# A four-block attention and feed-forward kernel on Trainium2: layer 6's context products between layer 5's stages, and layer 5's last two stages among layer 6's first softmax units

## The chip, the cores and the metric

The kernel is one program on one core of a Trainium2 chip. The metric is the device time of one execution in microseconds. Engines are named as in the profile: PE (TensorE, with PEld for its weight loads), DVE (VectorE), ACT (ScalarE), POOL (GpSimd) and SP (SyncE, which here only issues transfers). Each engine runs its own instructions strictly in the order in which the program lists them, and waits at semaphores for the others.

## What is computed

Four blocks act on x (4 x 512 x 128, fp32) and a context (4 x 77 x 128). Each adds a gated attention and then a gated feed-forward part; the kernel numbers these eight parts as layers 0 to 7. The change lies between layer 5 and layer 6:

```
# layer 5: three cycles of a small network on LN(x), all per sequence
gf  = global_net(mean over rows of LN(x))
out = LN(x)
for _ in range(3):
    tf = sigmoid(gelu(gelu(gelu(out@w1+b1)@w2+b2)@w3+b3)@w4+b4)   # stages 0 to 3
    out = out + (0.1 + ar*(0.7*gf + 0.3*tf - 0.5)*2) * twist(out) # stage 4 and couple
x = x + tanh(g) * out
# layer 6: attention with 16 heads of 8 channels on the 77 context rows
Q = LN(x)@wq.T + bq;  K = ctx@wk.T + bk;  V = ctx@wv.T + bv
x = x + tanh(g) * (softmax(mask(Q K.T / sqrt(8))) V @ wo.T + bo)
```

K and V of layer 6 depend on the context alone, not on x.

## The kernel before, in words

The four sequences are worked on in two passes of the whole program ("pairs"), with two sequences s = 0 and 1 in each. Activations are held as four tiles of 128 rows per sequence.

**The list of steps.** schedule() (line 127) writes out one list of steps by hand. Every engine runs through that list in order and issues its own part of each step, so the place of a step in the list is its place on every engine. No cost or due time is computed anywhere.

**PSUM slots.** Products land in six slots: S0 and S1 (two banks each), T0 and T1, G0 and G1 (one bank each); in the code they are 0 to 5. Four rotors (line 116) hand them out in the order of the list: `big` gives S0, S1 in turn, `turn` T0, T1, `gen` G0, G1, and `wide` S0, S1, T0, T1. The rotors do not know of each other. On TensorE `take(i)` (line 734) waits until all earlier contents of slot i have been read out:

```python
            def take(i):

                used[i] += 1
                pe.wait_ge(*free[i].value(used[i]))
```

**Layer 5.** cycle(s, n) (line 351) is stage n % 5 of cycle n // 5 of sequence s, written (s, cycle, stage) below. Stages 0 to 3 are, for each half of 256 columns, one product (two fp32 instructions) and one ScalarE activation. Stage 4 is the product for the twist over all 512 columns, followed by `couple` on VectorE for both halves: three operations of 256 columns each (lines 1816, 1818, 1824), which update `cur` = `kh`, a tile with both sequences' state. The two sequences run interleaved, the second seven stages behind: the loop at line 372 issues stage n of sequence 0 and stage n - 7 of sequence 1 for n = 4 to 21. cycle_out transposes the result back, and VectorE adds it to x. Then norm_stats, norm_apply and norm_turn of layer 6 normalise x and transpose it.

**Layer 6's products.** project_context(6, s) multiplies the context with the keys' weights into a `gen` slot (two instructions of 77 columns) and a repeated context with the values' weights into a `big` slot (five products, ten instructions). VectorE evicts the keys with their bias (line 1777) and the values in two multiplications by a 0/1 block pattern (line 1780), whose second frees the big slot; GpSimd spreads the keys by head (line 1383). project_queries(6, s) is one product of 512 columns and one VectorE eviction (line 1799). Before, the keys of sequence 0 went into `qh` and those of sequence 1 into `kh`, that is into layer 5's state of sequence 0, so that they had to come after its last use.

**The units.** small_attention (line 166) runs 16 softmax units (sequence, tile, half of the heads). Unit k issues its scores into a big slot, then VectorE's less_max (a maximum, line 1531, and a subtraction that frees the slot, line 1535); with delays of one to five units follow ScalarE's exp, the transposes of the probabilities (turn_probs), the product with the values (mix_values), turn_heads and project_tile. Its argument `between` names steps that are issued ahead of unit k's scores. SyncE waits for the second context products of layer 6 (line 702) before it loads the next pair's context.

Of the kernel before, what the change touches and what calls it, by code (L numbers as in the profile page):

```python
# [20 lines left out]
KEYS = 77  # L21
# [105 lines left out]
def schedule():  # L127

    big, turn, gen = Rotor(S0, S1), Rotor(T0, T1), Rotor(G0, G1)
# [3 lines left out]
    def do(kind, *args):  # L133
        st.append((kind, args))

    def norm_stats(l, s):
        do("norm_stats", l, s)

    def norm_apply(l, s):
        if l == 2:  # L140
            do("norm_again", l, s)
        do("norm_apply", l, s)
        if l in BIASED:
            do("add_bias", l, s)
# [5 lines left out]
    def norm_turn(l, s):  # L150
        do("norm_turn", l, s, gen())
# [119 lines left out]
    n, half, rest = len(units), H1 * NT, values1(1) + [("shifts1", 1)]  # L271
# [97 lines left out]
                        20: (lambda: do("global_net", 0, 3, None), lambda: cycle(0, 3))})  # L369

    late = 7
    for n in range(4, 15 + late):
        if n < 15:
            cycle(0, n)
        if n == 4:
            norm_stats(5, 1)
        if n == 5:
            norm_apply(5, 1)
        if n == 6:
            norm_turn(5, 1)  # L380
        if n == 15:
            do("cycle_out", 0, gen())
        if n >= late:
            cycle(1, n - late)
        if n == 16:
            norm_stats(6, 0)
        if n == 17:
            norm_apply(6, 0)
        if 0 <= n - late < 4:
            do("global_net", 1, n - late, gen() if n - late < 3 else None)  # L390
        if n == 19:
            norm_turn(6, 0)
        if n == 20:
            do("project_context", 6, 0, gen(), big())
            do("project_queries", 6, 0, turn(), turn())

    small_attention(6, {1: (lambda: do("cycle_out", 1, gen()),), 2: (lambda: norm_stats(6, 1),),
                        3: (lambda: norm_apply(6, 1),), 5: (lambda: norm_turn(6, 1),),
                        6: (lambda: do("project_context", 6, 1, gen(), big()), lambda: do("project_queries", 6, 1, gen(), turn())),
                        15: (lambda: norm_turn(7, 0),), 16: (lambda: hidden(7, 0, 0, 0, 1), lambda: do("logits", 7, 0, gen())),  # L400
                        17: (lambda: gates(7, 0, 0), lambda: hidden(7, 0, 0, 2)),
                        18: (lambda: gates(7, 0, 1), lambda: hidden(7, 0, 0, 3), lambda: hidden(7, 0, 1, 0)),
# [8 lines left out]
def program(nc, dram, known):  # L411
# [3 lines left out]
    with ExitStack() as ctx:  # L415
# [85 lines left out]
        rot, cur = [qh, kh], kh  # L501
# [10 lines left out]
        kbd = [arenaD[:, 1280 * s:1280 * s + 16 * KEYS].rearrange("p (h k) -> p h k", h=16) for s in range(NS)]  # L512
# [112 lines left out]
        def tensor_did(*event):  # L625

            for i in range(6):
                if (it[0],) + event in known[f"filled_{i}"]:
                    return filled[i].at(*event)
            return unknown(filled[0], event)  # L630
# [25 lines left out]
        def parts_free(eng, l, s, e):  # L656

            n = PARTED.index((l, s, e))
            if n >= 2 and PARTED[n - 2][0] == l:
                eng.wait_ge(*tensor_did("hid", *PARTED[n - 2], FT - 1))  # L660

        def load_rows(eng, s):
            eng.wait_ge(scattered[s].sem, it[0] * 128 + 128)
# [701 lines left out]
        def _(pool):  # L1365
# [13 lines left out]
            def project_context(l, s, i, n):  # L1379

                need(pool, "block")
                pool.wait_ge(*reader_did("kv", l, s))
                nc.gpsimd.tensor_tensor(kbd[s], rot[s][:, 1, 0:KEYS].unsqueeze(1).broadcast_to([128, 16, KEYS]),
                                        W["block"].unsqueeze(2).broadcast_to([128, 16, KEYS]), ALU.mult)\
                    .then_inc(*heads_ready.mark(l, s))

# [62 lines left out]
        def _(dve):  # L1449
# [318 lines left out]
            def project_context(l, s, i, n):  # L1768
                dve.wait_ge(*filled[i].at("kv", l, s))
                rt = rot[s]  # L1770
                kk = rt[:, 1, 0:KEYS]
                if l == 4:
                    v.tensor_tensor(kk, slot(i, KEYS), W["cos"][:, 0:KEYS], ALU.mult)
                    link(v.tensor_tensor(rt[:, 1, 128:128 + KEYS], slot(i, KEYS, at=KEYS), W["sin"][:, 0:KEYS], ALU.mult))
# [230 lines left out]
```

## Time and profile before

| what | value |
|---|---|
| median of 3 runs | 1453.79 us (1448.89 to 1456.07) |
| profiled execution, its own time | 1444.35 us |
| its span | 1442.2 us |
| TensorE products | 1297.7 us busy, 90% of the span |
| VectorE, ScalarE, GpSimd | 758.5, 704.5 and 204.1 us busy |
| mean granted TensorE clock | 0.976 of full speed |

The span runs from the first to the last instruction, and the profiled execution's own time is 2.15 us longer. Stages of the two pairs lie about 703 us apart: the stretch of the change is at 538 to 590 us and again at 1241 to 1293 us. In a timeline, consecutive instructions of one kind are merged into one row with their count, so a row's start is that of the first of them.

### The profile page before, as it was taken

What the parts mean: (1) busy time and instruction counts of PE and PEld (TensorE: products, weight loads), DVE (VectorE), ACT (ScalarE), POOL (GpSimd) and SP (SyncE); (2) the same over time, 40 slices, a digit from 0 to 9 for tenths busy, and PEclk for the clock granted to TensorE, in tenths of its full rate; (3) what the DMA queues carried; (4) which work ended last, traced back from release to release, by engine and by line L of the source; (5) the groups of instructions that cost most, each with busy time, mean ns of one, the idle gap of its engine ahead of it and who ended that gap; (6) DMA issues with size and microseconds to landing.
All of it is one profiled execution on the core that took longest, in us unless ns stands there. A gap on an engine that the chain in (4) does not pass through costs nothing.

```text
span 1442.2 us, 23241 instructions
## 1 busy us (share of the span) xinstructions
PE 1297.7 (90%) x8544; PEld 1067.1 (74%) x8544; DVE 758.5 (53%) x2099; ACT 704.5 (49%) x1486; POOL 204.1 (14%) x195
## 2 busy tenths in 40 slices
PE   6888999999988688999979989999998958899998
PEld 5587577778986565879957856777788847577898
DVE  3775444565415656754356835445643356476532
ACT  2763455555533254454547535555553424544553
POOL 1044100002141001100011620000203220020000
PEclk8999999999999799999999999999999979999999
DMA  6000000004484000000000000000228430000000
GB/s 271 1 1 1 1 1 1 1 1 159 133 269 158 6 0 1 6 1 2 15 15 1 1 1 1 1 1 1 67 94 284 158 123 1 1 1 1 1 8 8
DMA packets 30381, 64.87 MB, mean 45 GB/s; under 512 B 3358, under 2 KB 19008, under 8 KB 29504
## 3 DMA queue, kind: packets, MB, share of 16 engines
q1 hardware_dynamic: 15728, 49.56, 9.7%
q10 hardware_dynamic: 12496, 9.62, 2.1%
q0 software_dynamic: 2048, 4.20, 0.9%
q8 instruction: 72, 1.18, 0.3%
q14 instruction: 37, 0.30, 0.1%
HBM read 54.33 MB, written 9.04 MB: 44 GB/s over the span
## 4 chain that ended last, share of the span: by engine, by line
PE 75%; DVE 11%; DMA 4%; ACT 4%; POOL 3%; issue 3%; SPq 0%; DVEq 0%; POOLq 0%; ACTq 0%
PE psum L745 65%; PE psum L779 10%; DMA outs_dram<-arenaC 2%; DVE xn L1491 1%; ACT arenaB L1131 1%; ACT arenaA L1131 1%; POOL rows_dram L1404 1%; POOL arenaA L1412 1%; DMA rows_dram<-xn,row_at 1%; DVE arenaA L1818 1%; DVE nmax L1531 1%; DMA arenaA<-rows_dram 1%; POOL rs L1368 1%; DVE stat L1467 1%; DVE x L1753 1%
## 5 line engine op out<-in xcount | busy, mean ns | idle before, releaser
L1131 ACT ACTIVATE arenaB<-psum 128x512 f32<-128x512 f32 x448 | 168.0, 426 | 115.7 <-PE psum L779 114.6
L1131 ACT ACTIVATE arenaA<-psum,vec 128x512 f32<-128x512 f32 (+1 forms) x208 | 125.3, 614 | 152.9 <-PE psum L745 152.4
L745 PE MATMUL psum<-arenaD,arenaB 128*128 128x128 f32 (+2 forms) x1440 | 186.7, 278 | 7.0 <-ACT arenaB L1131 6.8
L745 PE MATMUL psum<-moe,arenaA 128*128 128x128 f32 x1504 | 183.9, 276 | 3.3 <-DVE gt L1640 1.6
L745 PEld LDWEIGHTS psum<-moe,arenaA 128*128 128x128 f32 x1504 | 177.4, 193 | 8.4 <-issue 3.8
L1131 ACT ACTIVATE probs<-probs,nmax 128x589 f32<-128x589 f32 x128 | 100.8, 787 | 168.0 <-DVEq L1614 167.9
L745 PEld LDWEIGHTS psum<-arenaD,arenaB 128*128 128x128 f32 (+1 forms) x1440 | 173.6, 194 | 12.0 <-ACT arenaB L1131 11.1
L1611 DVE CUSTOM_DVE_ANT_0 probs<-psum,shift 128x589 f32<-128x589 f32 x128 | 98.7, 771 | 154.4 <-PE psum L745 152.8
L779 PE MATMUL psum<-w_first,probs 128*128 128x128 f32 (+2 forms) x1120 | 161.3, 275 | 11.7 <-POOL probs L1430 7.4
L1368 POOL TENSOR_TENSOR rs<-ve,half_power 128x4 f32<-128x4 f32 x36 | 37.4, 1039 | 843.4 <-DVE ve L1473 839.7
L779 PEld LDWEIGHTS psum<-w_first,probs 128*128 128x128 f32 (+2 forms) x1120 | 131.3, 144 | 33.9 <-issue 21.4
L745 PE MATMUL psum<-seen,qh 128*128 128x512 f32 (+1 forms) x512 | 154.4, 424 | 1.6 <-ACT qh L1131 1.6
L745 PEld LDWEIGHTS psum<-seen,qh 128*128 128x128 f32 x512 | 87.3, 191 | 65.5 <-issue 62.3
L1131 ACT ACTIVATE arenaA<-psum 128x512 f32<-128x512 f32 (+2 forms) x130 | 57.4, 449 | 93.2 <-PE psum L745 48.6
L1131 ACT ACTIVATE probs<-probs 128x616 f32<-128x616 f32 x96 | 68.8, 717 | 69.3 <-DVE probs L1535 58.5
L1588 DVE SCALAR_TENSOR_TENSOR x<-psum,gt,x 128x128 f32<-128x128 f32 x128 | 36.0, 343 | 107.5 <-PE psum L745 107.5
L745 PEld LDWEIGHTS psum<-arenaA,arenaB 128*128 128x128 f32 (+1 forms) x640 | 78.1, 192 | 9.7 <-issue 9.2
L1531 DVE TENSOR_REDUCE nmax<-psum 128x8 f32<-128x616 f32 x80 | 63.5, 794 | 39.4 <-PE psum L745 39.4
L745 PE MATMUL psum<-arenaA,arenaB 128*128 128x128 f32 (+1 forms) x640 | 83.7, 278 | 0.0
L745 PE MATMUL psum<-parts 128*128 128x512 f32 x336 | 83.4, 398 | 0.0
L1622 DVE TENSOR_SCALAR probs<-probs,rsum 128x589 f32<-128x589 f32 x128 | 68.1, 532 | 4.5
L779 PE MATMUL psum<-w_first,xn 128*128 128x128 f32 x160 | 30.3, 289 | 44.5 <-DVE xn L1547 30.5
(230 smaller groups left out, 2009.3 us busy)
## 6 DMA issues: line engine op xcount, KB each, us to landing
moe<-in_w_moe_dram SPq DMA_DIRECT2D x60, 512.0 KB, 5.0
moe<-in_w_moe_dram SPq DMA_DIRECT2D x2, 4096.0 KB, 13.9
moe<-in_w_folds_dram SPq DMA_DIRECT2D x3, 1024.0 KB, 10.7
outs_dram<-arenaC ACTq DMA_DIRECT2D x8, 384.0 KB, 3.6
rows_dram<-arenaB SPq DMA_DIRECT2D x2, 960.0 KB, 17.0
arenaA<-rows_dram SPq DMA_DIRECT2D x2, 768.0 KB, 5.5
arenaA<-rows_dram ACTq DMA_DIRECT2D x2, 768.0 KB, 7.0
w_l<-in_w_l_dram ACTq DMA_DIRECT2D x1, 1500.0 KB, 12.9
```

The costliest lines, as they stand in the source:

```text
L745: return nc.tensor.matmul(out, lhsT, rhs, start=start, stop=stop, skip_group_check=shared)
L779: return nc.tensor.transpose(out, in_, ident[0:p, 0:p])
L1131: return nc.scalar.activation(out, in_, func, **kw)
L1368: nc.gpsimd.tensor_tensor(rs[:, s, int(again), :], ve[:, s, int(again), :], half_power[:, 0:NT], ALU.pow)\
L1404: nc.gpsimd.indirect_dma_start(dram[f"rows{s}"], bass.IndirectOffsetOnAxis(ap=row_at[:, s, n:n + 1], axis=0), xn[:, s, n % NT, :], None).t ...
L1412: nc.gpsimd.indirect_dma_start(back[s][:, 128 * n:128 * n + 128], None, dram[f"outs{s}"], bass.IndirectOffsetOnAxis(ap=row_at[:, s, n:n + ...
L1467: last = v.bn_stats(stat[:, s, t, :], x[:, s, t, :])
L1491: last = v.tensor_scalar(xn[:, s, t, :], x[:, s, t, :], mv[:, s, t, 0:1], rs[:, s, r, t:t + 1], ALU.subtract, ALU.mult)
L1531: v.tensor_reduce(nmax[:, k % 4, :], sc, AX, ALU.max, negate=True).then_inc(*unit_max.mark(l, s, hf, t))
L1588: last = v.scalar_tensor_tensor(x[:, s, t, :], slot(i, 128, at=128 * t), gt[:, s, 7, E * t + e:E * t + e + 1], x[:, s, t, :], ALU.mult, AL ...
L1611: v.tensor_tensor_reduce(row_probs[k % 4], slot(i, 589), shift1[:, s, t, h:h + 1].broadcast_to([128, 589]), 1.0, 3.0e38, ALU.add, ALU.min, ...
L1622: v.tensor_scalar(row_probs[k % 4], row_probs[k % 4], rsum[:, k % 4, 1, 0:1], None, ALU.mult)\
```

## The change

The second sequence's keys get a place of their own beside the first's (keys_at), outside layer 5's state. With it both project_context steps of layer 6 move up: s = 0 from the loop's n = 20 to n = 9, s = 1 from unit 6 to n = 13. The loop ends two stages earlier, and stages 13 and 14 of sequence 1 (its last activation stage and its last twist with couple) are issued ahead of the scores of units 0 and 1. In the list below that, norm_turn(6, 0) and project_queries(6, 0) come one stage earlier, and cycle_out(1) and the normalisation of sequence 1 one unit later, with project_queries(6, 1) at unit 7.

```diff
--- before.py
+++ after.py
@@ -369,7 +369,7 @@
                         20: (lambda: do("global_net", 0, 3, None), lambda: cycle(0, 3))})
 
     late = 7
-    for n in range(4, 15 + late):
+    for n in range(4, 13 + late):
         if n < 15:
             cycle(0, n)
         if n == 4:
@@ -378,6 +378,8 @@
             norm_apply(5, 1)
         if n == 6:
             norm_turn(5, 1)
+        if n in (9, 13):
+            do("project_context", 6, n // 13, gen(), big())
         if n == 15:
             do("cycle_out", 0, gen())
         if n >= late:
@@ -388,15 +390,15 @@
             norm_apply(6, 0)
         if 0 <= n - late < 4:
             do("global_net", 1, n - late, gen() if n - late < 3 else None)
+        if n == 18:
+            norm_turn(6, 0)
         if n == 19:
-            norm_turn(6, 0)
-        if n == 20:
-            do("project_context", 6, 0, gen(), big())
             do("project_queries", 6, 0, turn(), turn())
 
-    small_attention(6, {1: (lambda: do("cycle_out", 1, gen()),), 2: (lambda: norm_stats(6, 1),),
-                        3: (lambda: norm_apply(6, 1),), 5: (lambda: norm_turn(6, 1),),
-                        6: (lambda: do("project_context", 6, 1, gen(), big()), lambda: do("project_queries", 6, 1, gen(), turn())),
+    small_attention(6, {0: (lambda: cycle(1, 13),), 1: (lambda: cycle(1, 14),),
+                        2: (lambda: do("cycle_out", 1, gen()),), 3: (lambda: norm_stats(6, 1),),
+                        4: (lambda: norm_apply(6, 1),), 6: (lambda: norm_turn(6, 1),),
+                        7: (lambda: do("project_queries", 6, 1, gen(), turn()),),
                         15: (lambda: norm_turn(7, 0),), 16: (lambda: hidden(7, 0, 0, 0, 1), lambda: do("logits", 7, 0, gen())),
                         17: (lambda: gates(7, 0, 0), lambda: hidden(7, 0, 0, 2)),
                         18: (lambda: gates(7, 0, 1), lambda: hidden(7, 0, 0, 3), lambda: hidden(7, 0, 1, 0)),
@@ -659,6 +661,10 @@
             if n >= 2 and PARTED[n - 2][0] == l:
                 eng.wait_ge(*tensor_did("hid", *PARTED[n - 2], FT - 1))
 
+        def keys_at(l, s):
+
+            return rot[s][:, 1, 0:KEYS] if l == 4 else rot[0][:, 1, 128 * s:128 * s + KEYS]
+
         def load_rows(eng, s):
             eng.wait_ge(scattered[s].sem, it[0] * 128 + 128)
             for h, (a, b) in enumerate(((0, 3), (3, TILES3))):
@@ -1380,7 +1386,7 @@
 
                 need(pool, "block")
                 pool.wait_ge(*reader_did("kv", l, s))
-                nc.gpsimd.tensor_tensor(kbd[s], rot[s][:, 1, 0:KEYS].unsqueeze(1).broadcast_to([128, 16, KEYS]),
+                nc.gpsimd.tensor_tensor(kbd[s], keys_at(l, s).unsqueeze(1).broadcast_to([128, 16, KEYS]),
                                         W["block"].unsqueeze(2).broadcast_to([128, 16, KEYS]), ALU.mult)\
                     .then_inc(*heads_ready.mark(l, s))
 
@@ -1768,7 +1774,7 @@
             def project_context(l, s, i, n):
                 dve.wait_ge(*filled[i].at("kv", l, s))
                 rt = rot[s]
-                kk = rt[:, 1, 0:KEYS]
+                kk = keys_at(l, s)
                 if l == 4:
                     v.tensor_tensor(kk, slot(i, KEYS), W["cos"][:, 0:KEYS], ALU.mult)
                     link(v.tensor_tensor(rt[:, 1, 128:128 + KEYS], slot(i, KEYS, at=KEYS), W["sin"][:, 0:KEYS], ALU.mult))
```

The stretches of the list that change, as the rotors then number the slots (last numbers of a step; project_context has the keys' slot and then the values'). After:

```
cycle (0,1,4) 4   couple x2   project_context(6,0) 5, 0   cycle (1,0,2) 0 and 1   global_net   cycle (0,2,0) 2 and 3
cycle (1,0,3) 0 and 1   cycle (0,2,1) 2 and 3   cycle (1,0,4) 5   ...
cycle (0,2,3) 0 and 1   project_context(6,1) 4, 1   cycle (1,1,1) 2 and 3   cycle (0,2,4) 5   couple x2   ...
norm_turn(6,0)   cycle (1,2,2)   project_queries(6,0)   cycle (1,2,3)   scores 0   less_max 0
cycle (1,2,4)   couple x2   scores 1   less_max 1   exp 0   cycle_out(1)   scores 2   less_max 2 ...
```

Before, the last two lines read:

```
cycle (1,2,2)   norm_turn(6,0)   cycle (1,2,3)   project_context(6,0)   project_queries(6,0)   cycle (1,2,4)   couple x2
scores 0   less_max 0   cycle_out(1)   scores 1   less_max 1   exp 0   scores 2   less_max 2 ...
```

From the scores of the eighth unit on, both lists are the same, slots included.

## Rows read from the trace of the kernel before

**Rows 1.** The page: busy time of TensorE, and the chain that ended last by engine

```profile
PE 1297.7 (90%) x8544; PEld 1067.1 (74%) x8544; DVE 758.5 (53%) x2099; ACT 704.5 (49%) x1486; POOL 204.1 (14%) x195
...
PE 75%; DVE 11%; DMA 4%; ACT 4%; POOL 3%; issue 3%; SPq 0%; DVEq 0%; POOLq 0%; ACTq 0%
```

**Rows 2.** Busy time by stretch: us, then busy us (count) per engine, clock, DMA, GB/s

```profile
538.00:553.00 15.00, 12.42 (x48) 8.01 (x47) 7.09 (x19) 9.28 (x23) 0.00 (x0) 1.00 0.01 2
```

**Rows 3.** Timeline, TensorE: start us, us, what [idle before <- releaser]

```profile
539.46 1.03 PE L745 MATMUL psum<-arenaA,w_l 128*128 128x256 f32 x4
...
540.73 0.70 PE L745 MATMUL psum<-kh,w_l 128*128 128x256 f32 x2
541.91 0.70 PE L745 MATMUL psum<-kh,w_l 128*128 128x256 f32 x2 [0.48 <-DVE kh L1824]
```

**Rows 4.** Timeline, VectorE, behind the couple steps of (0, 1)

```profile
541.78 0.21 DVE L1809 TENSOR_SCALAR gl<-gl,scaled 128x1 f32<-128x1 f32 x1
```

**Rows 5.** Timeline, context products and queries of layer 6, and their evictions

```profile
562.83 0.34 PE L745 MATMUL psum<-ctx_pad,w_l 128*128 128x77 f32 x2
...
563.01 1.32 PE L745 MATMUL psum<-w_l,ctx_again 128*128 128x128 f32 x10
...
563.21 0.30 DVE L1777 TENSOR_SCALAR qh<-psum,vec 128x77 f32<-128x77 f32 x1 [1.79 <-PE psum L745]
...
564.17 1.02 PE L745 MATMUL psum<-seen,w_l 128*128 128x512 f32 x2
564.37 0.89 DVE L1780 TENSOR_TENSOR arenaD<-psum,w_first 128x320 f32<-128x320 f32 x2 [0.86 <-PE psum L745]
...
565.23 0.75 DVE L1799 TENSOR_SCALAR qh<-psum,vec 128x512 f32<-128x512 f32 x1
```

**Rows 6.** Timeline, from stage (0, 2, 3) to the eighth scores, three engines

```profile
548.02 1.89 PE L745 MATMUL psum<-arenaA,w_l 128*128 128x256 f32 x8
...
548.65 0.91 ACT L1131 ACTIVATE arenaA<-psum,scaled 128x256 f32<-128x256 f32 x2
...
549.75 1.02 PE L745 MATMUL psum<-kh,w_l 128*128 128x512 f32 x2
...
553.06 0.66 PE L779 MATMUL psum<-w_first,kh 128*128 128x128 f32 x4 [1.43 <-DVE kh L1824]
...
561.47 0.66 PE L779 MATMUL psum<-w_first,xn 128*128 128x128 f32 x4 [0.52 <-DVE xn L1491]
...
566.04 1.30 PE L745 MATMUL psum<-arenaD,qh 128*128 128x308 f32 x4
...
568.38 0.79 DVE L1531 TENSOR_REDUCE nmax<-psum 128x8 f32<-128x616 f32 x1
...
568.52 0.66 PE L779 MATMUL psum<-w_first,kh 128*128 128x128 f32 x4 [0.89 <-DVE kh L1824]
...
569.92 0.74 DVE L1555 SCALAR_TENSOR_TENSOR x<-psum,gates_t,x 128x512 f32<-128x512 f32 x1
...
570.34 1.20 PE L745 MATMUL psum<-arenaD,qh 128*128 128x308 f32 x4
...
578.98 1.20 PE L745 MATMUL psum<-arenaD,qh 128*128 128x308 f32 x4
...
580.50 0.80 DVE L1531 TENSOR_REDUCE nmax<-psum 128x8 f32<-128x616 f32 x1 [0.29 <-PE psum L745]
...
584.38 1.20 PE L745 MATMUL psum<-arenaD,qh 128*128 128x308 f32 x4
...
587.53 1.20 PE L745 MATMUL psum<-arenaD,qh 128*128 128x308 f32 x4
```

**Rows 7.** Timeline, the same stretch in the second pair

```profile
1244.89 0.70 PE L745 MATMUL psum<-kh,w_l 128*128 128x256 f32 x2 [0.48 <-DVE kh L1824]
```

**Rows 8.** Busy time by stretch, after the second dispatch of layer 3's rows

```profile
470.00:475.00 5.00, 0.00 (x0) 0.00 (x0) 2.17 (x8) 0.00 (x0) 0.95 (x1) 0.50 0.10 26
480.00:485.00 5.00, 4.31 (x19) 3.88 (x19) 2.18 (x5) 2.01 (x5) 0.00 (x0) 0.50 0.00 0
```

## The prediction

> **What bounds the kernel now.** I read the page first (TensorE's share, then the chain that ended last), then the busy times by stretch around the change, then the timeline instruction by instruction in the stretch that the diff reorders. TensorE is busy for 90% of the span and carries 75% of the chain that ended last [rows 1]. In layer 5's stages it is not full: of 15 us it was busy 12.42, at full granted clock [rows 2]. The time in those stages is set by short chains from engine to engine (product, activation, two or three VectorE operations, next product), so a step placed there costs only what the idle time beside it can't take. Behind them, in layer 6's softmax units, one step follows the other on TensorE without gap: 3.15 us from one unit's scores to the next [rows 6]. Whatever shift the reordered stretch leaves is therefore carried to the end, and it comes twice, once for each pair of sequences. The second pair shows the same stretch with the same pattern [rows 7].
>
> The change moves three things: the products of the first sequence of layer 6 (stage 20 to stage 9), those of the second (unit 6 to stage 13), and two cycle stages behind the first scores. All times below are those of the first pair.
>
> **Part 1, the first context products.** In their new place they follow the product for the twist of (0, 1), and the next step is cycle (1, 0, 2). They take slot S0, the next one of the big rotor. Cycle (1, 0, 2) takes S0 too, the next one of the wide rotor. TensorE's take waits until every earlier reader of a slot is done, and S0's reader is now VectorE with its two block multiplications (L1780). VectorE works in order: in the list they stand behind both couple steps of (0, 1), which before end where the next VectorE instruction starts, at 541.78 [rows 4]. Then the keys' eviction and the two multiplications: 0.30 + 0.89 us [rows 5], 1.2 us with the gap between them, so S0 comes free at about 543.05. Before, cycle (1, 0, 2) started at 539.46 [rows 3]. It starts 3.6 us later. Given back is the idle time in front of cycle (0, 2, 0)'s second half: the first half starts at 540.73 and takes 0.43 (four such halves fill the 1.73 us from 548.02 to 549.75 [rows 6]), so it ended at 541.16, and the second waited for the couple step until 541.91 [rows 3]: 0.75 us. Net **+2.85 us**. TensorE's own cost of the products, 1.34 us (562.83 to 564.17 [rows 5]), lies inside this wait. GpSimd's multiplication of the keys by head (L1383) runs while GpSimd has no other step, and its reader, the first scores, comes some 20 us later: nothing.
>
> **Part 2, the second context products.** They stand behind cycle (0, 2, 3) and take slot S1, which that stage's second half has just filled. The keys' product uses another slot and goes ahead, but the values' five must wait for the activation: both halves end at 548.65 + 0.91 = 549.56, so they start at 549.62. They issue for 1.16 us (563.01 to 564.17 [rows 5]) and end at 550.78. Before, TensorE was through the eight half-width instructions of stage (0, 2, 3) and (1, 1, 1) at 549.75, of which the first half, up to 548.88, comes ahead of the new place. So everything behind it, the twist of (0, 2) included, is 550.78 - 548.88 = **+1.9 us** later. The idle 1.43 us at 553.06 [rows 6] does not help: it is a wait for the couple step that hangs on this same twist. VectorE has the keys and the multiplications done at about 551.9, before the delayed twist lands, so it adds nothing.
>
> **Part 3, the end of layer 5 and the first units.** Counted without the two delays. Layer 6's transposes of its input start at 561.47 as before, since they wait for VectorE's normalised rows, whose chain is not touched [rows 6]. One cycle stage and then the queries follow, where one stage and the context products were: the queries start at 562.83 instead of 564.17. Their eviction starts 1.1 us later and takes 0.75 (565.23 against 564.17 [rows 5]), so the first scores start at 564.75 instead of 566.04: 1.3 us gained. But then VectorE takes the first unit's maximum and subtraction ahead of the couple steps. Scores to VectorE 1.52 us (578.98 to 580.50, the only unit here that VectorE waited for), the two operations 1.54 us (568.38 to 569.92), couple steps 2.5 us (from the end of the queries' eviction, 565.98, to 568.38): they end at 570.45. Cycle_out's transposes, which wait for them, started at 568.52 and now start at 570.5. They are 2.0 us later, but the second scores (1.33 us) are already done, so the third start 0.65 us later than the 570.34 of before [rows 6]. TensorE stands idle for some 2.1 us there.
>
> From here TensorE is full. Up to the seventh scores (584.38 before) the same steps remain less the second context products and the second queries: 1.34 + 0.86 (twice the 0.43 of a half) = 2.20 us. So they start at 584.38 + 0.65 - 2.20 = 582.83. One unit later (3.15 us) the second queries come, at 585.98; they take a slot that VectorE's project_tile frees, behind the seventh maximum and subtraction: 582.83 + 1.52 + 1.54 + 0.35 = 586.25 (0.35 is an estimate, between nothing and the 0.74 us that such an operation took on four times the columns, at 569.92). With 0.86 for the queries the eighth scores start at 587.15, against 587.53 [rows 6]: **-0.35 us**. Bounds of this term: -2.7 if all of the moved TensorE work left a full engine and nothing else waited, +0.65 if the later units give nothing back. I take the walk's value, since each step has its own row.
>
> SyncE's load of the next pair's context waits for the second context products, so its two transfers start earlier. What stands behind them on that queue waits for layer 7's output: nothing.
>
> **Sum.** 2.85 + 1.9 - 0.35 = 4.4 us for a pair, 8.8 us for the kernel. The profiled execution took 1444.35 us (span 1442.2), and would take 1453.15. The median of the three runs shown is 1453.79, 0.65% above it. I forecast the median: **1462.6 us, +0.6%**. For the two delays, the lower bound is that the slots cost nothing and only TensorE's own work counts: 1.34 - 0.75 = 0.6 and 1.34; the upper is no idle time recovered: 3.6 and 1.9. With part 3's bounds a pair lies between -0.8 and +6.2 us.
>
> **A rule that speaks for it.** The trace shows two regimes side by side, TensorE 83% busy in the cycle stages and full in the units [rows 2, 6]. The Trainium skill (Perfetto Trace Analysis, Optimization Strategy) says that performance may be improved by interleaving regimes in which different engines are the most contended. Taken by itself it would put the moved 2.7 us of TensorE work in idle time and give about -5 us for the kernel; this is the second rival below.
>
> **Rivals.**
> (a) *No change to speak of:* the slot waits are shorter than I read them, for example because the stages have slack that I have not counted, and the lower bounds hold: 0.6 + 1.34 - 0.35 = 1.6 us a pair, +3.2 us, 1457. For it: all engines have idle time in this stretch [rows 2]. Against it: the wait for S0 follows from the order of the list alone.
> (b) *Faster:* the place is the full TensorE in the units. If the couple steps do not fall behind the first maximum, cycle_out keeps its start and part 3 gives the full 2.7 us, with early costs of 0.6 + 0 (the second products hidden in the 1.43 us at 553.06). That is -2.1 us a pair, 1449.5. It turns on VectorE: it decides from the point where part 3's couple steps end before 568.5. Against it is VectorE's fixed order.
> (c) *Much slower, by the clock.* TensorE stands idle here for two new gaps of 2.1 to 2.3 us (540.8 to 543.05, and ahead of cycle_out). After a long idle stretch the granted clock was 0.50, which is the 1.2 GHz level [rows 8], and stage work then takes twice as long. Priced as 10 us at half clock a pair, an estimate by the stretch up to 485 us, still at 0.50 some 10 us after TensorE's 5 idle us [rows 8]: +5 us a pair, +10 in all, 1472.6. Against it: gaps of 1.43 us leave the clock at 1.00 [rows 2, 6], and the full half-clock stretch came after more than 5 us of idle. The Trainium skill (TensorE: Matmul & The Clock Gate, "Why this matters for your kernels") warns that long idle gaps between bursts of products put the clock back to the half rate; the trace agrees for the long gap [rows 8] and shows no fall for gaps up to 1.43 us, and nothing in it lies between.
> That the change does not do what it says is no rival of weight: the keys get a place of their own, so nothing hinders the early start.
>
> **Chances and range.** My forecast 0.68, (a) 0.18, (b) 0.08, (c) 0.06. A measurement of this kernel can tell about 0.5%, 7.3 us, from no change. The forecast of 8.8 lies close to that: I give two thirds to three quarters of it, with most of (c), to slower, the rest and all of (a) to same, along with a part of (b). Slower 0.56, same 0.38, faster 0.06. The range reaches from 1452.5 (below (a), into a small part of (b), with a median that moves by a few us) to 1470 (upper bounds, 2 x 6.2 = +12.4, and some of (c)).
>
> **What the changed profile would show.** Part 1: TensorE idle some 2.3 us before the product of cycle (1, 0, 2), released by VectorE's arenaD (L1780). Part 2: a gap of about 0.55 us inside the second context products, released by ScalarE, and the couple step of (0, 2) 4.7 us later than before. Part 3: cycle_out waiting about 2 us for the couple step, the first maximum ahead of it, and the eighth scores 4.4 us later than before. I am wrong if cycle (1, 0, 2) starts within 1.5 us of the context products' start, or if the units from the eighth on start less than 2 us or more than 6 us later; and in another way, if the granted clock falls below 1.00 between 540 and 575 us.

## The result, and the profile after

The changed kernel takes 1468.12 us (median of 4 runs, 1466.36 to 1471.18) against 1451.34 us (4 runs) for the kernel before: the ratio is 1.0124, 95% interval 1.0098 to 1.0151, that is 14 to 22 us slower. The forecast was 1462.6, slower by 8.8 us; the time lies in the range given (1452.5 to 1470), but the slowdown is about twice the one forecast.

The page of the kernel after (in the engines' code its lines are six higher, so L745 is now L751), busy times and the chain by engine, beside [rows 1]:

```profile
PE 1312.7 (89%) x8544; PEld 1078.6 (73%) x8544; DVE 758.7 (52%) x2099; ACT 706.3 (48%) x1486; POOL 204.4 (14%) x195
...
PE 72%; DVE 12%; DMA 5%; ACT 4%; POOL 3%; issue 3%; SPq 0%; DVEq 0%; POOLq 0%; ACTq 0%
```

The products are the same 8544. TensorE's share of the chain falls from 75% to 72%, and VectorE's and the transfers' rise by 1% each; where TensorE waits for VectorE is read from the timeline below.

I measure a pair on TensorE from the product for the twist of (0, 1) to the eighth unit's scores. Before, that is 538.50 to 587.53, 49.03 us, and 49.04 in the second pair, with the clock at 1.00 (before, both pairs; columns: stretch, us, busy us per engine, granted clock, DMA):

```profile
538.50:587.53 49.03, 43.02 (x224) 31.76 (x223) 33.64 (x87) 22.89 (x50) 9.09 (x6) 1.00 0.02 4
1241.47:1290.51 49.04, 43.01 (x224) 31.77 (x223) 33.66 (x87) 22.89 (x50) 9.10 (x6) 1.00 0.00 1
```

The busy times of the same stretch after, first and second pair, and of the part of each with a low clock:

```profile
544.54:601.17 56.63, 45.51 (x224) 33.48 (x223) 33.74 (x89) 24.67 (x52) 9.10 (x6) 0.94 0.02 4
1260.91:1317.41 56.50, 44.71 (x225) 33.03 (x223) 33.75 (x89) 24.63 (x52) 9.11 (x6) 0.97 0.00 1
569.00:577.00 8.00, 6.30 (x16) 3.39 (x14) 2.36 (x12) 2.97 (x6) 2.27 (x2) 0.57 0.00 0
1265.40:1269.30 3.90, 3.88 (x10) 2.81 (x11) 0.21 (x1) 1.55 (x4) 1.49 (x1) 0.56 0.00 0
```

The stretch is 7.6 and 7.5 us longer, and in each pair the clock fell once to 0.50: within 569 to 577, and within 1265.4 to 1269.3, the latter right behind the new wait of part 1. Before, it did not fall in this stretch.

Part 1 of the prediction in the timeline after (TensorE and VectorE, first pair; it starts 6.04 us later than before):

```profile
544.54 1.12 PE L751 MATMUL psum<-kh,w_l 128*128 128x512 f32 x2
...
545.50 0.34 PE L751 MATMUL psum<-ctx_pad,w_l 128*128 128x77 f32 x2
...
545.68 1.32 PE L751 MATMUL psum<-w_l,ctx_again 128*128 128x128 f32 x10
...
547.81 0.29 DVE L1783 TENSOR_SCALAR qh<-psum,vec 128x77 f32<-128x77 f32 x1
...
548.02 0.88 DVE L1786 TENSOR_TENSOR arenaD<-psum,w_first 128x320 f32<-128x320 f32 x2
...
549.04 1.10 PE L751 MATMUL psum<-arenaA,w_l 128*128 128x256 f32 x4 [2.04 <-DVE arenaD L1786]
...
553.08 1.02 PE L751 MATMUL psum<-seen,w_l 128*128 128x512 f32 x2
```

Stage (1, 0, 2) stood for 2.04 us, with the multiplications that empty S0 named as releaser, and began 4.50 us behind the twist; before it was 0.96 us (538.50 to 539.46, [rows 3]). The twist of (1, 0) (553.08) comes 8.54 us behind that of (0, 1), against 5.67 before.

Part 2 (ScalarE's activations of (0, 2, 3), then TensorE up to cycle_out of the first sequence):

```profile
557.56 0.91 ACT L1137 ACTIVATE arenaA<-psum,scaled 128x256 f32<-128x256 f32 x2
...
557.79 0.34 PE L751 MATMUL psum<-ctx_pad,w_l 128*128 128x77 f32 x2
...
558.52 1.38 PE L751 MATMUL psum<-w_l,ctx_again 128*128 128x128 f32 x10 [0.39 <-ACT arenaA L1137]
...
559.74 1.03 PE L751 MATMUL psum<-arenaA,w_l 128*128 128x256 f32 x4
...
560.60 1.02 PE L751 MATMUL psum<-kh,w_l 128*128 128x512 f32 x2
...
563.91 0.66 PE L785 MATMUL psum<-w_first,kh 128*128 128x128 f32 x4 [1.43 <-DVE kh L1830]
```

The values' products wait 0.39 us for ScalarE behind the keys' product, and the wait of 1.43 us for the couple step in front of cycle_out is as long as in [rows 6]: it moved along with everything, it hid nothing.

Part 3 (TensorE, second pair, where the clock was at 1.00 in this part): layer 6's transposes, queries, last activation stage, first scores, cycle_out, third scores, the transposes of the heads, second queries, eighth scores:

```profile
1290.29 0.66 PE L785 MATMUL psum<-w_first,xn 128*128 128x128 f32 x4 [1.79 <-DVE xn L1497]
...
1291.65 1.11 PE L751 MATMUL psum<-seen,w_l 128*128 128x512 f32 x2
...
1293.69 1.10 PE L751 MATMUL psum<-arenaA,w_l 128*128 128x256 f32 x4 [0.94 <-DVE qh L1805]
...
1294.63 1.20 PE L751 MATMUL psum<-arenaD,qh 128*128 128x308 f32 x4
...
1300.33 0.66 PE L785 MATMUL psum<-w_first,kh 128*128 128x128 f32 x4 [2.04 <-DVE kh L1830]
...
1300.82 1.20 PE L751 MATMUL psum<-arenaD,qh 128*128 128x308 f32 x4
...
1310.54 0.33 PE L785 MATMUL psum<-w_first,xn 128*128 128x128 f32 x1 [0.49 <-DVE xn L1553]
...
1316.47 1.10 PE L751 MATMUL psum<-seen,w_l 128*128 128x512 f32 x2 [0.23 <-DVE x L1569]
...
1317.41 1.20 PE L751 MATMUL psum<-arenaD,qh 128*128 128x308 f32 x4
```

Two waits here are in no step of the prediction: 0.94 us ahead of the last activation stage, for VectorE's eviction of the queries (L1805), and 0.49 us ahead of the heads' transposes (1310.54).

### The profile page after: what moved, and what is told of

Same layout as the page of the kernel before. It is cut to its first block, busy times and chain, and to the rows that moved or that the text cites. A ratio compares the mean times of both kernels' runs of the same rounds, so it can differ in the third digit from the quotient of the medians.

```text
span 1469.0 us, 23243 instructions
## 1 busy us (share of the span) xinstructions
PE 1312.7 (89%) x8544; PEld 1078.6 (73%) x8544; DVE 758.7 (52%) x2099; ACT 706.3 (48%) x1486; POOL 204.4 (14%) x195
## 4 chain that ended last, share of the span: by engine, by line
PE 72%; DVE 12%; DMA 5%; ACT 4%; POOL 3%; issue 3%; SPq 0%; DVEq 0%; POOLq 0%; ACTq 0%
PE psum L751 63%; PE psum L785 9%; DMA outs_dram<-arenaC 2%; DVE xn L1497 2%; DVE nmax L1537 1%; DMA moe<-in_w_folds_dram 1%; DVE probs L1541 1%; ACT arenaA L1137 1%; ACT arenaB L1137 1%; POOL rows_dram L1410 1%; POOL arenaA L1418 1%; DVE stat L1473 1%; DMA rows_dram<-xn,row_at 1%; DVE arenaA L1824 1%; DMA arenaA<-rows_dram 1%
## 5 line engine op out<-in xcount | busy, mean ns | idle before, releaser
L751 PE MATMUL psum<-arenaD,arenaB 128*128 128x128 f32 (+2 forms) x1440 | 187.6, 279 | 7.0 <-ACT arenaB L1137 6.8
L751 PE MATMUL psum<-moe,arenaA 128*128 128x128 f32 x1504 | 186.3, 278 | 3.3 <-DVE gt L1646 1.6
L751 PEld LDWEIGHTS psum<-moe,arenaA 128*128 128x128 f32 x1504 | 179.8, 195 | 8.4 <-issue 3.8
L751 PEld LDWEIGHTS psum<-arenaD,arenaB 128*128 128x128 f32 (+1 forms) x1440 | 174.9, 195 | 12.1 <-ACT arenaB L1137 11.1
L785 PE MATMUL psum<-w_first,probs 128*128 128x128 f32 (+2 forms) x1120 | 161.9, 275 | 11.7 <-POOL probs L1436 7.4
L751 PE MATMUL psum<-seen,qh 128*128 128x512 f32 (+1 forms) x512 | 154.4, 424 | 1.6 <-ACT qh L1137 1.6
L751 PEld LDWEIGHTS psum<-seen,qh 128*128 128x128 f32 x512 | 87.3, 191 | 65.5 <-issue 62.3
L751 PEld LDWEIGHTS psum<-arenaA,arenaB 128*128 128x128 f32 (+1 forms) x640 | 78.1, 192 | 9.7 <-issue 9.2
L751 PE MATMUL psum<-arenaA,arenaB 128*128 128x128 f32 (+1 forms) x640 | 83.7, 278 | 0.0
L751 PE MATMUL psum<-parts 128*128 128x512 f32 x336 | 83.3, 397 | 0.0
```

The costliest lines, as they stand in the source:

```text
L751: return nc.tensor.matmul(out, lhsT, rhs, start=start, stop=stop, skip_group_check=shared)
L785: return nc.tensor.transpose(out, in_, ident[0:p, 0:p])
```

## Experiments

All ratios are of the whole kernel to the kernel before, with 95% intervals. "tw10" is the start of the twist product of (1, 0) and "sc8" that of the eighth scores, both in us behind the twist of (0, 1), for the two pairs; "falls" counts the stretches at half clock between the twist of (0, 1) and sc8 in the two pairs. The times of stretches and the falls are those of one profiled execution of each kernel.

| kernel | tw10 | sc8 | falls | ratio |
|---|---|---|---|---|
| before | 5.67, 5.68 | 49.03, 49.04 | 0 | 1 |
| the change | 8.54, 10.13 | 56.63, 56.50 | 2 | 1.0124 (1.0098 to 1.0151) |
| x1: products alone | 10.14, 8.54 | 53.30, 51.97 | 2 | 1.0054 (1.0037 to 1.0071) |
| x2: tail order alone | 5.68, 5.68 | 54.07, 54.18 | 2 | 1.0088 (1.0060 to 1.0116) |
| x3: change, later slots | 7.43, 7.44 | 52.13, 53.77 | 1 | 1.0074 (1.0047 to 1.0101) |
| x4: x3 with the old tail | 7.44, 7.43 | 49.33, 49.16 | 2 | 1.0002 (0.9987 to 1.0017) |
| x5: change, queries in G | 10.13, 10.14 | 56.84, 57.40 | 4 | one run: 1467.82 us against 1447.88 |
| x7: change, filled waits | 8.54, 8.54 | 54.97, 56.03 | 1 | 1.0113 (1.0081 to 1.0144) |
| x8: x4, filled | 7.49, 7.49 | 49.00, 48.99 | 0 | 1.0002 (0.9986 to 1.0017) |
| x9: before, filled | 5.68, 5.67 | 49.12, 49.10 | 0 | 1.0010 (0.9995 to 1.0026) |
| x10: x8, apart | 6.87, 6.87 | 48.37, 48.38 | 0 | 0.9990 (0.9978 to 1.0002) |
| x11: change, next stage in T | 7.17, 7.18 | 53.52, 53.53 | 0 | one run: 1459.91 us against 1449.30 |
| x12: x10, one fill less | 6.44, 6.43 | 47.95, 47.95 | 0 | 0.9994 (0.9980 to 1.0009) |
| x13: x12 without fills | 6.43, 6.43 | 47.95, 47.94 | 0 | 0.9996 (0.9982 to 1.0009) |

### The two halves of the change apart (x1, x2)

x1 is the change with the order of before behind stage 13. x2 has the change's order there, but the context products right ahead of the queries:

```diff
 x1, against the change
-    for n in range(4, 13 + late):
+    for n in range(4, 15 + late):
...
+        if n == 19:
+            norm_turn(6, 0)
+        if n == 20:
+            do("project_queries", 6, 0, turn(), turn())
...
 x2, against the change
-        if n in (9, 13):
-            do("project_context", 6, n // 13, gen(), big())
...
         if n == 19:
+            do("project_context", 6, 0, gen(), big())
             do("project_queries", 6, 0, turn(), turn())
...
-                        7: (lambda: do("project_queries", 6, 1, gen(), turn()),),
+                        7: (lambda: do("project_context", 6, 1, gen(), big()), lambda: do("project_queries", 6, 1, gen(), turn())),
```

> The context products in their new places, the rest of the order as before (parts 1 and 2 of the prediction alone). I measure a pair from the twist of (0, 1) to the eighth scores: 49.03 us before, 56.5 to 56.6 with the whole change. Theory of the slots: TensorE's waits for S0 and S1 cost 2.85 + 1.9 us here too, and the full TensorE of the units gives back at most the 2.7 us of products that left it, so 51.1 to 52 us for the stretch, +4 to +6 us for the kernel (+0.3 to +0.4%). Rival, that only TensorE's own work counts in the early place: 0.6 + 1.34 - 2.7, so 48.3 us and -1.5 us for the kernel.

> The order of part 3 alone (first maximum and subtraction ahead of the last couple steps, queries ahead of the last activation stage, one unit more delay for the second sequence), with the context products right ahead of the queries of their sequence as before. Theory that this order costs by itself, through VectorE's first maximum ahead of the couple steps and the queries' slot T0, which the stage behind them takes too: about 52 us for the stretch, +6 us for the kernel (+0.4%). Rival, that the order is neutral as the prediction had it (-0.35 us, of which the products' removal is part): 49 to 50 us, at most +2 us for the kernel.

x1, busy times of the stretch in both pairs:

```profile
538.77:592.07 53.30, 45.05 (x225) 32.91 (x224) 33.55 (x87) 23.10 (x50) 9.11 (x6) 0.97 0.02 4
1249.34:1301.31 51.97, 44.49 (x225) 32.70 (x223) 33.55 (x87) 22.95 (x50) 9.10 (x6) 0.97 0.00 1
```

The products alone make the kernel 0.54% slower, where 0.3 to 0.4% were expected. In the second pair the early part was at full clock and tw10 is 8.54 as in the change; that stretch of 51.97 lies in what the theory of the slots gave (51.1 to 52) and the rival's 48.3 is out. Its fall of the clock comes later, ahead of layer 6's transposes, and moved them by only some 0.3 us (they start 28.12 us behind the twist, where 22.97 of before and the two waits of 4.81 make 27.78). So the moved products cost 2.6 to 2.9 us a pair, and some 2 of the 4.8 us of the two waits come back behind them.

x2, the wait ahead of cycle_out, the third scores behind it, and the stretch:

```profile
580.88 0.67 PE L784 MATMUL psum<-w_first,kh 128*128 128x128 f32 x4 [2.04 <-DVE kh L1829]
...
581.37 2.24 PE L750 MATMUL psum<-arenaD,qh 128*128 128x308 f32 x4
...
546.37:600.44 54.07, 44.67 (x224) 33.19 (x223) 33.61 (x89) 24.54 (x53) 8.20 (x6) 0.97 0.00 1
```

The order alone makes the kernel 0.88% slower and costs 5.0 and 5.1 us a pair; the rival of a neutral order falls. The expectation was about 52 us and 0.4%, less than half of what the kernel lost. About 1.7 us of the 5 is the clock: behind the new wait of 2.04 us it is 3.53 us from the third scores to the fourth (581.37 to 584.90), against 1.87 in the second pair after (1300.82 to 1302.69). The other 3.4 us are the order's own, so at full clock the stretch comes near the 52 us. The two halves add up to 1.0142, about the 1.0124 of the whole.

### The slots (x3, x11, x5)

x3 moves both products behind the activation stage that takes S0 and S1. x11 leaves every step in place and lets only the wide rotor skip two slots. x5 takes the queries out of T0.

```diff
 x3, against the change (x4: the same, with the old tail of x1)
-        if n in (9, 13):
-            do("project_context", 6, n // 13, gen(), big())
...
             do("global_net", 1, n - late, gen() if n - late < 3 else None)
+        if n in (9, 14):
+            do("project_context", 6, n // 14, gen(), big())
 x11, against the change
             cycle(0, n)
+        if n == 12:
+            wide(), wide()
...
             do("project_context", 6, n // 13, gen(), big())
+        if n == 9:
+            wide(), wide()
 x5, against the change
-            do("project_queries", 6, 0, turn(), turn())
+            do("project_queries", 6, 0, gen(), turn())
...
-                        7: (lambda: do("project_queries", 6, 1, gen(), turn()),),
+                        7: (lambda: do("project_queries", 6, 1, turn(), turn()),),
```

> The change with every step in the same place; only the wide rotor skips two slots behind the first context products (and two more three stages later, where it costs nothing), so that the next stage takes T0 and T1 and the one behind it meets S0. Theory of the slot: TensorE goes straight on with stage (1, 0, 2), 1 us instead of 3.4 us after the values' products start, waits for VectorE's multiplications only ahead of stage (0, 2, 0), for about 1 us instead of 2.04, and the twist of (1, 0) starts 1.6 us instead of 2.85 us later than before at full clock (that is 7.3 us after the twist of (0, 1), against 8.54 in the change and 5.67 before). If it is the products' length or VectorE's work that delays the stage, 8.5 us as in the change.

x11, the values' products, stage (1, 0, 2), the global net, stage (0, 2, 0):

```profile
541.26 1.32 PE L755 MATMUL psum<-w_l,ctx_again 128*128 128x128 f32 x10
542.41 1.03 PE L755 MATMUL psum<-arenaA,w_l 128*128 128x256 f32 x4
543.37 0.38 PE L755 MATMUL psum<-gl,w_l 32*128 32x1 f32 x2
544.63 1.10 PE L755 MATMUL psum<-kh,w_l 128*128 128x256 f32 x4 [0.88 <-DVE arenaD L1790]
```

Stage (1, 0, 2) follows the products at once (1.15 us behind their start), and the wait of 2.04 us became one of 0.88 a stage later. tw10 is 7.17 (7.3 expected, 8.54 in the change). With the same products and the same VectorE work, other slot numbers give back 1.4 us a pair. That shows the slot as the cause of part 1: where it still has to be waited for, one stage later, 1.5 us are left of the 2.87. This run had the clock at 1.00 throughout, so 53.5 + 1.4 = 54.9 us is the change's stretch at full clock.

> The change with both context products one stage further (as in the run with the old tail, whose stretch from the twist of (0, 1) to the eighth scores took 49.2 to 49.3 us), and with the change's own tail. Theory of the slots: only the two early waits shrink, from 2.85 + 1.9 us to 0.6 + 0.3 us, so the stretch falls from 54.9 us (the change without its half-clock time) to 51 us at full clock and to at most 53 us with a fall of the clock in it; the kernel is 0.5 to 0.7% slower than before. Rival, that a product costs its own length wherever it stands in layer 5: 52.8 us at full clock.

tw10 fell from 8.54 to 7.43, and the twist of (0, 2) from 16.06 to 13.01 us. The first pair, at full clock, took 52.13: 2.8 us under the 54.9, where 3.9 were expected, and nearer to the rival's 52.8 than to my 51. The second pair, with a fall of the clock in it, took 53.77, over the 53 that were expected at most. What is missing stands in x3's timeline, global net and then the keys' product:

```profile
545.90 0.38 PE L751 MATMUL psum<-gl,w_l 32*128 32x1 f32 x2
547.03 0.42 PE L751 MATMUL psum<-ctx_pad,w_l 128*128 128x77 f32 x2 [0.75 <-DVE arenaA L1824]
```

The keys' product stands for 0.75 us behind VectorE: it takes G0, in which the twist of (0, 1) still waits for the couple step. This is a third slot conflict, and x3 itself brought it in.

> The change, with the first queries in a one-bank slot that the next stage does not take (the second queries take that one's turn, so the slots agree again afterwards). In the change the last activation stage stood for 0.93 us behind the queries' eviction. If it is the slot that does this, that idle time is gone, the stage follows the queries on TensorE at once, and the stretch is about 1 us shorter at the same clock. If the wait is for something else (the activations of the stage ahead), it stays.

x5, queries, last activation stage, first scores:

```profile
568.32 1.11 PE L751 MATMUL psum<-seen,w_l 128*128 128x512 f32 x2
569.26 1.03 PE L751 MATMUL psum<-arenaA,w_l 128*128 128x256 f32 x4
570.27 1.30 PE L751 MATMUL psum<-arenaD,qh 128*128 128x308 f32 x4
```

The stage follows the queries at once (0.94 us against 2.04 behind them), and the first scores come 1.95 us behind the queries instead of the 2.98 of the second pair after. So the wait came from T0. That the stretch becomes 1 us shorter, as expected, can't be read here: two falls of the clock in each pair hide it in the total.

### The clock (x7, x8, x9)

The fills are products of constants that nothing reads, in the slot that the waiting step takes anyway (x8 and x9 have them, with 256 columns each, ahead of the stages 0 that wait for a couple step, and one ahead of layer 5's and 6's transposes and of cycle_out). In x7:

```diff
+            def fill(i, n):
+                for _ in range(n):
+                    mm(slot(i, 512), W["ones"], W["cos"])
...
             def cycle_out(s, i):
+                take(i)
+                if s == 1:
+                    fill(i, 2)
                 pe.wait_ge(*coup_ready.at(s, 2, 1))
-                take(i)
```

> The change, with products of constants that nothing reads put into three of TensorE's waits: one (about 0.86 us) ahead of the first values' products, two ahead of layer 6's first transposes, two ahead of cycle_out of the second sequence, each into the slot that the waiting step takes anyway. If the new idle gaps bring the half clock, the granted clock stays at 1.00 from the twist of (0, 1) to the eighth scores in both pairs, and the stretch takes 54.6 to 55 us instead of 56.5 to 56.6; the waits for the slots stay. If the clock falls for another reason, the stretch stays at 56.5 or grows.

```profile
536.99:591.96 54.97, 47.37 (x235) 33.89 (x234) 33.78 (x89) 24.42 (x53) 9.11 (x6) 1.00 0.01 4
1251.18:1307.21 56.03, 48.62 (x235) 34.68 (x233) 33.76 (x89) 24.45 (x52) 9.11 (x6) 0.97 0.00 1
```

The first pair kept the clock at 1.00 and took 54.97, as expected; the second fell once, behind waits that were not filled (for the couple steps of (1, 1)), and took 56.03. So the expectation held in one pair of two. Against 54.97 the change's two falls cost 1.7 and 1.5 us (56.63 and 56.50), and the one in x7 1.1 us.

> The context products moved as in the change but each one stage further, behind the activation stage that takes S0 and S1, so that the next user of the slot is two stages away; the tail in the order of before. Theory of the slots: the waits shrink to 0.6 and about 0.3 us, 2.7 us leave the units, so the stretch takes 47 to 47.5 us (49.03 before) and the kernel is 3 to 4 us faster than before (-0.2 to -0.3%). Theory that any product placed between layer 5's stages delays its chain by its own length: 49 us, no change. Theory that the clock decides: half clock somewhere in the stretch, over 50 us.

> The version with later products and the old tail, whose stretch took 49.2 to 49.3 us with one fall to half clock in each pair, plus products of constants in TensorE's waits of layer 5 (256 columns each, one or two per wait, in the slot that the waiting step takes anyway, each shorter than the wait). If the fall follows from the idle time, it is gone: clock 1.00 in the stretch, 47.0 to 47.5 us, and the kernel 3 to 5 us faster than before (0.2 to 0.35%). If the clock falls whatever TensorE does here, 49.2 or more and no change of the time.

> Control: the kernel before with the same fill products and nothing else. Its stretch had no fall of the clock in the one execution profiled, so the stretch stays at 49.0 us; the kernel is unchanged, or up to 0.2% faster if other executions of before do have such falls. If fill products cost time themselves, the stretch is longer than 49.2 us.

The expectations of x4 and x8 were wrong, for the stretch and for the kernel's time. x4 took 49.33 and 49.16 with one fall a pair, its kernel the same as before (1.0002). I put this down to the clock; x8 held it at 1.00 in both pairs and took 49.0 all the same. In x4 the fall lay ahead of the transposes, which wait for VectorE's normalised rows in any case: they began 25.36 us behind the twist in x4 and 25.09 in x8, 0.3 us apart. A fall costs little where the step behind it waits for another engine. What had eaten the gain was the G0 conflict of x3: tw10 is 7.43 to 7.49 in x4 and x8 too, and x12 below, without that conflict, takes 1.05 us less than x8. The control x9 shows that the fills cost less than 0.1 us a pair where a wait covers them.

### Three slots apart (x10, x12, x13)

```diff
 against x8
             cycle(1, n - late)
+        if n in (9, 14):
+            do("project_context", 6, n // 14, gen(), big())
...
-        if n in (9, 14):
-            do("project_context", 6, n // 14, gen(), big())
```

> The filled version with later products, with the first context products one step earlier again: behind the activation stage that takes S0 and S1, but ahead of the global net's third product, so that their keys take G1, which is free, instead of G0, in which the twist of (0, 1) still waits for the couple step. There the keys' product stood for 0.75 us with VectorE as its releaser. If that third slot conflict is what cost the filled version its gain, the stretch falls from 49.0 to 47.8 us, the twist of (1, 0) comes 0.6 us instead of 1.8 us later than before, and the kernel is 2 to 3 us faster than before (0.15 to 0.2%). If a product placed in layer 5 costs its own length in any case, the stretch stays at 49.0 us.

The stretch is 48.37, so a little more than half of the expected gain came: tw10 is 6.87, not 6.3. The kernel's ratio of 0.9990 is 1.4 us where 2 to 3 were expected, and its interval (0.9978 to 1.0002) does not tell it from nothing. One fill stood where no wait was left. x12 drops that one, x13 drops all.

> The version of three slots apart without the one fill product (0.43 us) ahead of the second half of stage (0, 2, 0), where its trace shows no wait left to fill: there the fill stood on TensorE's path and the twist of (1, 0) came 6.87 us after that of (0, 1). Expected: 6.4 us, a stretch of 47.9 us instead of 48.4 (49.03 before) at clock 1.00, and the kernel 2.2 us faster than before (0.15%), at the edge of what five rounds can tell. If the stretch stays at 48.4, something behind it on the path (VectorE's couple steps) had been the later one.

> The same places without any fill product. If the fills do nothing but hold the clock: the same 47.9 us where the clock stays at 1.00, and up to 1.7 us more in a pair in which it falls in front of a full TensorE (less where a wait for another engine follows). The kernel then between 0.2% faster than before and the same as before. If the falls come without regard to idle time, the filled version has as many of them.

Both stretches take 47.95 us, as expected, with and without fills. x13:

```profile
538.00:585.95 47.95, 43.16 (x225) 32.19 (x224) 33.60 (x87) 22.97 (x50) 9.10 (x6) 1.00 0.02 4
1245.12:1293.06 47.94, 43.16 (x224) 32.17 (x223) 33.58 (x87) 22.97 (x49) 9.09 (x6) 1.00 0.00 1
```

This is the change's idea without its slot conflicts and without its tail: 1.1 us a pair gained over before. In the kernel's time that is 2.2 us, 0.15%, and x12's and x13's intervals (0.998 to 1.001) do not tell it from nothing. No version that clearly beats the kernel before was found.

## Why the prediction was right or wrong

**What bounds it, and twice.** This was right: the shift of the stretch (7.6 and 7.5 us) comes in both pairs.

**Part 1, +2.85.** Measured +2.87 (8.54 against 5.67), S0 free 4.50 us behind the twist against the 4.55 worked out. x11 shows that it is the slot.

**Part 2, +1.9.** Measured +1.94 (twist of (0, 2) at 16.06 instead of 11.25, less 2.87). The bound "nothing, if the 1.43 us hid it" was tried in x13 with the products behind stage (1, 1, 2): there it costs 0.36 us (cycle_out 3.67 us behind the twist of (0, 2), 3.31 before).

**Part 3, -0.35: this step failed.** At full clock (x11, whose parts 1 and 2 come to 3.44 us) the units' shift is 53.52 - 49.03 - 3.44 = +1.05, and with x7's first pair 54.97 - 49.03 - 4.81 = +1.13. That is outside the bounds given for the term (-2.7 to +0.65). The sentence that failed is "the first scores start at 564.75": it lets the last activation stage run beside the queries' eviction. The rotor gives both T0, so the stage waits for the eviction and the scores for the stage, 2.98 us from queries to scores instead of the 1.92 worked out (x5 removes it). I had looked for the next user of each slot that the moved products take, and not of the slots whose steps were only reordered. The other 0.4 us lie in the units of the second pair after: 0.25 between the third and the seventh scores (12.09 us against 11.84 worked out), where the heads' transposes waited 0.49 us for VectorE, and 0.18 between the seventh and the eighth (4.50 against 4.32). The rest of the step held: cycle_out came 5.70 us behind the first scores, 5.75 worked out, and TensorE waited 2.04 us for VectorE ahead of it, 2.1 worked out. The step's own sum was also a little off: 564.75 + 1.52 + 1.54 + 2.5 is 570.31 and not 570.45, and 586.25 + 0.86 is 587.11 and not 587.15. Added up as they stand, its rows give -0.6 us and not -0.35, further from what was measured.

**The clock, rival (c).** It was given 6 in 100 and 5 us a pair. It came in both pairs, at 1.7 and 1.5 us: the price, worked out from a long fall, was too high, and the chance too low. What was counted against it did not hold. The fall at 1265.4 followed a wait of 2.05 us (second pair after, stage (1, 0, 2)):

```profile
1265.42 1.83 PE L751 MATMUL psum<-arenaA,w_l 128*128 128x256 f32 x4 [2.05 <-DVE arenaD L1786]
```

And the prediction says that in the trace of before no gap lies between those of 1.43 us and the long one. That is a misreading. At 126 us TensorE has waited 2.34 us, and behind that wait the clock is at 0.50 (timeline, then busy times by stretch, before):

```profile
126.34 3.94 PE L745 MATMUL psum<-moe,arenaB 128*128 128x128 f32 x20 [2.34 <-ACT arenaB L1131]
...
127.20:130.40 3.20, 3.20 (x16) 3.20 (x16) 0.08 (x1) 0.00 (x0) 0.26 (x1) 0.50 0.02 5
```

The second pair shows the same at 832.26. Another wait of 2.16 us, at 40.22, has the clock at 1.00 behind it. So the trace of before had both outcomes for gaps as long as the new ones.

**Sum.** 2 x (2.87 + 1.94 + 1.13) = 11.9 us, and 2 x 1.6 = 3.2 us of clock make 15.1 of the 16.8 us between the medians (18 by the ratio). The forecast had 8.8: 3.0 us lack from part 3, 3.2 from the clock. The last 2 to 3 us lie outside the stretch and are not settled. In the two profiled executions the parts outside differ by 11.7 us (1344.1 and 1355.9), with more half clock in them after (0.62 against 0.72 mean clock from 468 to 504 us, in steps that the change does not touch). But these are single executions: that of before (1444.35) lies 7.0 us below its median, that of after (1471.18) 3.1 above. The same parts took 1350.4 us in x9, 1350.8 in x11 and 1359.1 in x2, so they vary among single executions by more than what is to be explained.

**The range and the signs.** At full clock a pair is 5.9 us longer, just inside the upper bound of 6.2, and the time lies in the range because its upper end allowed for that bound and for some of the clock. The wait for T0 is in none of its terms, so that part of the agreement is luck. Two of the signs of being wrong came: the eighth scores are 7.6 and 7.5 us later, over the 6 that were named, and the clock fell in the stretch. The signs of parts 1 and 2 came out nearly as forecast: 2.04 us of idle time for 2.3, a gap of 0.39 us for 0.55, and the couple step of (0, 2) 4.8 us later for 4.7.

**Rivals (a) and (b).** Both are out: the slots cost what the order of the list says, and the couple steps did fall behind the first maximum.

## What to carry to other kernels

When a step is moved between others that share a rotor of buffers, write out which slot each step gets and who empties it, for the moved steps and for every step whose neighbour has changed; a free engine is not enough, the next user of the slot must stand far enough behind that the reader has come by. Here, the variants included, five steps met such a neighbour (S0, S1, T0, G0, and the second queries' slot), and skipping two slots of a rotor moved no work and gave 1.4 us. VectorE work put ahead of a short chain that TensorE waits for delays that chain, even where the work had to be done in any case: with the first maximum and subtraction (1.54 us) ahead of the couple steps, TensorE's wait ahead of cycle_out grew from 0.89 to 2.04 us. And before a gap is counted as harmless for the clock, look through the whole trace for gaps of its length.

## What the runs showed of the hardware

The granted clock fell to 0.50 in this stretch in most variants, in TensorE's waits or right behind them, and at another place in the second pair than in the first of the same execution (tw10 of 8.54 and 10.13 in the change). With one profiled execution of each, the nine kernels without fills have 13 falls in their 18 pairs; but three of them, before, x11 and x13, have none, and x11 has the wait of 2 us ahead of cycle_out too. The four versions with layer 5's waits filled have none in 8 pairs. That waits bring the fall is thus likely, and what decides is not settled. The length of a single wait does not decide it: the changed kernel has two waits of 2.0 us in each pair, and a fall followed on one of the four; the fall of its first pair (569) came behind two waits of 1.04 and 0.54 us for couple steps, which the kernel before has too, without a fall. The Trainium skill (TensorE: Matmul & The Clock Gate, "Why this matters for your kernels") says to avoid long idle gaps between bursts; here a fall followed directly on a wait of 2.05 us (1265.4 after), and the first pair after has a wait as long (549.04) without one.

What a fall costs depends on the step behind it: 1.5 to 1.7 us in the change, but 0.2 to 0.3 in x4, where the step behind it waits for VectorE in any case (49.33 and 49.16 against 49.00 in x8).
